# A decoder layer on one Trainium2 core: the order of work at five seams

## The reference

```python
# 1: gated delta rule, 8 heads of 128, two key/value steps for each token
q, k, v = (silu(depthwise_conv4(x @ W.T)) for W in (Wq, Wk, Wv))
state = state * exp(g_t);  v_new = (v_t - k_t @ state) * beta_t
state = state + outer(k_t, v_new);  o_t = q_t @ state
o = rmsnorm(o) * o_norm_w * silu(x @ Wg.T);  x = layernorm(x + o @ Wo.T)
# 2: attention over a 128-row context, 16 heads, rope, a window of 8 keys
# 3: x = layernorm(x + (silu(x @ Wg8.T) * (x @ Wu8.T)) @ Wd8.T), weights dequantized from int32
```

## Time and profile before

| | |
|---|---|
| median of 3 runs | 1237.61 us (1236.98 to 1241.41) |
| profiled execution, its own time | 1236.63 us |
| profiled execution, span of the trace | 1234.6 us, 2.0 us less |
| mean granted TensorE clock | 0.979 |
| PE busy | 1155.6 us, 94% of the span |
| DVE, ACT, POOL busy | 815.0, 716.3, 500.0 us |
| chain that ended last | PE 76%, POOL 6%, DVE 5% |

### The profile page before, as it was taken

How to read it: one execution, slowest core, us unless ns; L and a number is a source line. 1 busy time by engine, 2 the same in 40 slices (tenths; PEclk the granted TensorE clock), 3 DMA queues, 4 the chain that set the end, 5 groups by cost and what they waited for, 6 DMA issues and landing times.

```text
span 1234.6 us, 30002 instructions
## 1 busy us (share of the span) xinstructions
PE 1155.6 (94%) x12192; PEld 794.6 (64%) x12192; DVE 815.0 (66%) x1454; ACT 716.3 (58%) x1212; POOL 500.0 (41%) x709
## 2 busy tenths in 40 slices
PE   6878799999999999999998889859999999999987
PEld 2434455555555555555555556648998988998976
DVE  4878767867768768668675565565666566655552
ACT  4667476767677676676775766533444444444433
POOL 2549575676575674773774811100001100001000
PEclk9899899999999999999998999989999999999999
DMA  3112311412323223243325422161211222111100
GB/s 116 44 38 64 94 49 47 114 55 61 105 57 86 72 60 89 75 130 87 102 60 144 152 61 71 46 232 21 67 44 44 50 51 69 48 44 45 32 17 9
DMA packets 134601, 88.05 MB, mean 71 GB/s; under 512 B 79264, under 2 KB 118048, under 8 KB 133568
## 3 DMA queue, kind: packets, MB, share of 16 engines
q1 hardware_dynamic: 133312, 85.93, 25.7%
q10 hardware_dynamic: 1152, 0.21, 0.1%
HBM read 54.77 MB, written 14.55 MB: 56 GB/s over the span
## 4 chain that ended last, share of the span: by engine, by line
PE 76%; POOL 6%; DVE 5%; SPq 3%; issue 3%; ACT 3%; DMA 3%; ACTq 0%; POOLq 0%; DVEq 0%
PE proj L466 20%; PE out L1484 5%; PE turned_v_chain L1484 4%; PE gram L481 4%; PE proj L1423 4%; PE proj L1542 4%; PE turned_v_chain L1550 4%; PE out L490 2%; PE gram L1458 2%; PE turned_v_chain L595 2%; PE decays L496 2%; DVE conv L986 2%; PE turned_v_chain L628 2%; POOL inverse L1194 2%; PE turned_v_chain L472 2%
## 5 line engine op out<-in xcount | busy, mean ns | idle before, releaser
L986 DVE SCALAR_TENSOR_TENSOR conv<-proj,kq_weights,conv 128x504 f32<-128x504 f32 (+2 forms) x261 | 190.6, 732 | 29.1 <-ACT conv L732 22.3
L466 PE MATMUL proj<-xT,vg_weights 128*128 128x512 f32 x384 | 189.0, 615 | 1.5 <-DMA vg_weights<-in_vg_w 1.4
L1781 POOL TENSOR_TENSOR rope<-rope_part,rope_part 128x512 f32<-128x512 f32 x32 | 40.1, 1272 | 371.0 <-DVE rope_part L1720 371.0
L986 DVE SCALAR_TENSOR_TENSOR conv<-proj,vg_weights,conv 128x504 f32<-128x504 f32 (+2 forms) x192 | 140.9, 734 | 47.7 <-ACT conv L732 42.8
L466 PE MATMUL proj<-xT,kq_weights 128*128 128x512 f32 x348 | 165.4, 601 | 0.4 <-DVE conv L986 0.4
L1194 POOL TENSOR_TENSOR inverse<-inverse,rank_one 128x30 f32<-128x30 f32 (+14 forms) x240 | 126.2, 526 | 18.8
L1191 POOL TENSOR_TENSOR rank_one<-inverse 128x30 f32<-128x30 f32 (+14 forms) x240 | 117.3, 489 | 15.9
L466 PEld LDWEIGHTS proj<-xT,vg_weights 128*128 128x128 f32 x384 | 68.8, 192 | 68.7 <-issue 62.6
L466 PEld LDWEIGHTS proj<-xT,kq_weights 128*128 128x128 f32 x348 | 62.9, 191 | 74.0 <-issue 71.1
L481 PEld LDWEIGHTS gram<-keys_q 128*64 128x64 f32 x896 | 59.1, 141 | 60.3 <-ACT keys_q L743 39.7
L1559 ACT ACTIVATE rstd<-rstd 128x1 f32<-128x1 f32 x48 | 9.7, 202 | 144.2 <-DVE rstd L1667 144.2
(11 more groups left out here) (244 smaller groups left out, 2463.2 us busy)
## 6 DMA issues: line engine op xcount, KB each, us to landing
kq_weights<-in_kq_w SPq DMA_DIRECT2D x32, 390.0 KB, 3.6
vg_weights<-in_vg_w SPq DMA_DIRECT2D x32, 390.0 KB, 4.0
o_scratch<-oT SPq DMA_DIRECT2D x32, 256.0 KB, 2.7
o_in<-o_scratch SPq DMA_DIRECT2D x16, 512.0 KB, 4.1
diagonal<-gram_decayed SPq DMA_DIRECT2D x128, 32.0 KB, 1.9
inverse<-inverse SPq DMA_DIRECT2D x32, 128.0 KB, 2.7
q_first<-rope SPq DMA_DIRECT2D x128, 32.0 KB, 1.9
q_second<-rope SPq DMA_DIRECT2D x128, 32.0 KB, 1.9
```

What stands on the lines that cost most here:

```text
L466: mm = e.matmul(bank(c, u)[:], w[:, (k * 3 + c % 3) * 128:(k * 3 + c % 3 + 1) * 128], xT[g][:, k, :], start=(k == 0), stop=(k == KD - 1))
L986: e.scalar_tensor_tensor(acc(c, u)[:, :, back:], src[:, :, 0:S - back], weights(c, u)[:, j:j + 1], acc(c, u)[:, :, back:], ALU.mult, ALU.a ...
L1781: e.tensor_tensor(turned[half][:].rearrange("p b r q -> p r b q"), parts[2 * half][:], parts[2 * half + 1][:], op).then_inc(s_turned, 1)
```

## The change

Nothing is added or taken away; instructions change places.

1. SP: `load(3)` is issued in slot 41 ahead of the FFN weights, no longer in the loop's first round.
2. Drain, PE: `norm` goes ahead of `chain_y`; in slot 41 `out(2)` goes ahead of `turn_v(0)`.
3. Slot 32, PE: the last `gram(1)` moves from ahead of `output` to behind the projection G.
4. Fill: on PE the projection Q goes ahead of `gram(0)`; on ACT `tap(K1)` goes ahead of the silu of Q, `tap(Q)` ahead of the silu of K1, and `square_q` to the end; on DVE the convolution of Q follows that of K1.
5. Slot 33, DVE: the gate and `oT` go ahead of `solve_norms` and of V0's convolution.

```diff
 SP, slot 41
+                        ahead["load"](3)
                         weights_after_chain()
 PE, slots 1 to 8
+                    e.wait_ge(s_conv[Q], 3 * ua)
+                    project(Q, ua)
                     e.wait_ge(s_silu[Q], ub + 1)
...
                     gram(0, ub)
-                    e.wait_ge(s_conv[Q], 3 * ua)
-                    project(Q, ua)
 PE, drain
+                    if s > U:
+                        norm(ud - 1)
                     if live(uc):
                         chain_y(uc)
-                    if s > U:
-                        norm(ud - 1)
...
+                    if s == last_slot + 1:
+                        ahead["out"](2)
                     if live(ud):
...
                         turn_v(0, ud)
-                    if s == last_slot + 1:
-                        ahead["out"](2)
...
-                    if live(ub):
+                    if live(ua):
                         e.wait_ge(s_gm, 4 * ub + 2)
                         gram(1, ub)
...
                         project(G, uc)
+                        if live(ub) and not live(ua):
+                            e.wait_ge(s_gm, 4 * ub + 2)
+                            gram(1, ub)
 ACT, slots 1 to 8
                         tap(K0, ua)
+                        tap(K1, ua)
                         silu(Q, ub, KQ[ub % 2][:, :, 0:S])
-                    square_q(ub)
-                    tap(K1, ua)
+                    else:
+                        tap(K1, ua)
                     wait(e, s_gram, 2 * (ua - 1))
                     silu(K0, ua, keys(0, ua))
+                    tap(Q, ua)
                     silu(K1, ua, keys(1, ua))
-                    tap(Q, ua)
+                    square_q(ub)
 DVE, fill
                         convolve(K1, ua)
+                        convolve(Q, ua)
...
-                    if s < LAG:
-                        convolve(Q, ua)
-                    elif live(ua):
+                    if s >= LAG and live(ua):
                         convolve(K0, ua)
 DVE, slot 33 (last_batch)
+                    if last_batch:
+                        solve_load(loading, 0)
+                        solve_load(loading, 1)
+                        gate_output()
+                        solve_norms(loading)
+                    if live(uc):
+                        convolve(V0, uc)
 SP, tile loop
-                        if live(u1 + 1):
+                        if live(u1 + 1) and u1 > AHEAD:
                             load(u1 + 1)
```

More of the change, by code:

```diff
@@ L1112, in vector, with gate_output @@
                     last_batch = loading is not None and s > U
-                    if last_batch:
-                        solve_load(loading, 0)
-                        solve_load(loading, 1)
-                        solve_norms(loading)
-                    if live(uc):
-                        convolve(V0, uc)
-                    if loading is not None and not last_batch:
-                        solve_load(loading, 0)
-                    if live(uo):
+                    def gate_output():
                         if s > U:
@@ L1129, in vector @@
                                                ALU.mult).then_inc(s_og, 1)
+                    if last_batch:
[5 more added lines that the diff above has]
+                        convolve(V0, uc)
+                    if loading is not None and not last_batch:
+                        solve_load(loading, 0)
+                    if live(uo) and not last_batch:
+                        gate_output()
                     if live(uc):
```

## The result

| | before | after |
|---|---|---|
| median of the executions timed side by side (4 each) | 1237.62 us (1236.98 to 1241.41) | 1224.14 us (1221.33 to 1228.82) |
| ratio, 95% interval | | 0.9889 (0.9852 to 0.9925) |
| timed a second time (17 and 6 executions), median | 1237.52 us | 1229.45 us, ratio 0.9923 (0.9901 to 0.9946) |
| all executions of this study, mean | 1237.8 us (63) | 1227.2 us (10) |
| profiled execution, span | 1234.6 us | 1219.5 us |

The change makes the kernel faster by about 10.6 us, the difference of the two means (8.6 to 12.6). The first four executions and the first trace of the changed kernel gained more than that; much of the surplus is TensorE's clock, as the experiments show.

The account below looks back on a forecast made before the run. Full slots are PE-bound; only idle PE in fill (12.5 us) and drain (24.0) can be gained. 4.9 + 1.4 + 2.1 + 3.3 = 11.7 us off 1236.6 gives 1225.0; range 1220.5 to 1231.5.

Parts of the forecast that it names:

- the sum with the clock lost everywhere: Whole kernel: with low clock in every term, 4.1 + 1.0 + 2.1 + 2.75 = 10.0 us gained, so 1226.7.
- Fill, 4.9 us: Fill up to the first solve: earlier `decayed(1)`, SP issues and slot 4 weights bring `solve_load` 4.1 to 5.7 us earlier.
- The rival that made the kernel slower: Fill: PE's wait per slot for Q's silu passes 2 us and the clock stays low; 1256.8 us, chance 0.03.
- Behind the first solve, 0: Fill, slots 6 to 8: POOL's elimination sets `steps` for slot 9, so PE waits about 1.3 us; nothing more gained.
- Slot 32, 0: Slot 32: `gram(1)`'s wait goes, but `chain_low` needs DVE behind POOL's elimination and `chain_high` the inverse's DMA; no gain.
- Slots 33 to 36, 1.4: Drain: earlier gate and `oT` remove PE's 1.98 us wait; gain 1.0 to 2.6 us, limited by POOL's last elimination.
- norm over W, 2.1: Slots 37 to 40: `norm` covers three of PE's waits for ACT's copy of W, 0.71 us each.
- All that PE gains in slots 34 to 36 is cut to POOL's 2.6: Slots 34 to 36: POOL's last elimination limits what PE gains there to 2.6 us.
- it probably pays the 1.65 of the low clock once: End of slot 36: PE's wait grows to nearly 3 us, probably costing 1.65 us of low clock once.
- the term for `W_scaled`: Slot 34: `W_scaled` comes 1.4 to 3.4 us earlier, taken as 2.3, from PE's lost wait and G's clock.
- Slot 41, 3.3: Slot 41: `out(2)` fills PE's 3.76 us wait for ACT's ln; gain 2.75 to 3.75 us.
- Tile 3's load, 0: Behind slot 41: `out(3)` waits for DVE's dequantizing, not its load; FFN weights issue about 1.2 us later, no gain.

Follow-up runs that it names:

- Twice Q: Changed kernel with slot 8's Q projection done twice, 1.88 us more PE work: median 1224.64 us, mean 1225.8.
- the move of `steps`: Changed kernel with unit 9's steps behind the first elimination, fill weights issued before the diagonals, and unit 31's `decayed(1)` and `gram(1)` moved: 1221.43 us, ratio 0.9867.
- the diagonals early: Changed kernel with unit 31's `gram(1)` back in its old place and DVE's `decayed(1)` ahead of `solve_turn`: 1221.89 us, ratio 0.9862.
- norm alone: Kernel before with only `norm` ahead of `chain_y` in the drain: 1238.20 us, ratio 0.9999.
- The gate alone: Kernel before with only slot 33's gate and `oT` ahead of `solve_norms`: 1233.82 us, ratio 0.9972.
- the changed kernel again: The changed kernel run once more without an edit, against the kernel before: 1229.45 us, ratio 0.9923.

## Why the prediction came out right, point by point

The mean of the changed kernel's ten executions is 1227.2, 1225.0 was forecast, and 1226.7 stood there as the sum with the clock lost everywhere. Half of the 2.2 us between, 1.2, is the starting point: the forecast took its 11.7 off one execution of 1236.6, and the mean of the kernel before is 1237.8. The fill and slot 41 held; the slots between fell short by 2.6 us. That the first median, 1224.14, lies within 1 us of the forecast is luck: this shortfall was covered by executions that kept more of their clock.

- **Fill, 4.9 us: right.** `solve_load` comes 5.9 us earlier on the mean of six traces against five (73.4, 79.2), the first chain 5.2 (128.9, 134.1). The chain was the one named: DVE's `decayed(1)`, SP's diagonals and constants, the weights. Against an old fill that kept its clock the gain is 4.1, the lower bound that was forecast; against one that lost it, as in the rows of the prediction, 6.9, above the upper bound of 5.7. The 2.8 between them are mostly clock at two places: 1.2 to 1.4 in slot 4, where the forecast had 1.65, and about 1.2 in slot 1, which stood in no term (Q there at 3.4 us, 2.3 in the two others). Two more pieces were too small: Q's tap was there at 43.4 and not 44.9, so SP's chain came 4.2 us earlier, not 3.4, and a regular slot became 0.34 shorter (9.61 us against 9.95), not 0.1 or 0.2. The rival that made the kernel slower did not come: PE's wait for the silu of Q stayed at 1.0 us in these slots.
- **Behind the first solve, 0: right in size, half right in cause.** Twice Q costs nothing, so PE does not bound there. But POOL's elimination is not what the chain waits for at the end, as the move of `steps` shows; `steps` of slot 9, in the middle of it, is. What I left out is the price of the longer wait: at 2.2 us it cost 1.6 or 1.7 us of clock in three of eight traces; the old fill, which hardly waits there, lost none in five.
- **Slot 32, 0:** not tested alone. The moved `gram` let `chain_low` start at 16.26 instead of 17.69 us from the slot's first `chain_y`, and PE then waited for `inverse`, as foretold. What I left out is the move's price on the other side: with `gram(1)` behind G the last diagonals come later, and DVE waits 3.34 us for them ahead of `solve_load` instead of 1.78. With the diagonals early this wait goes.
- **Slots 33 to 36, 1.4, and norm over W, 2.1: this is the step that failed.** "All that PE gains in slots 34 to 36 is cut to POOL's 2.6" fits the first two traces, 2.6 and 2.4 shorter than before (with the diagonals early it is 5.9), and "it probably pays the 1.65 of the low clock once" holds. Together with the W term they were to leave 3.5. Slots 32 to 39 took 133.6 us before and, in the five traces with all drain edits and nothing else in the drain, 134.5, 129.9, 131.9, 133.0 and 134.5, mean 132.8: 0.9 us. Three things failed. First, PE lost its 1.98 us wait for `oT` in slot 33, but waited there for `inverse` (1.0 to 3.0 us in all five) and for V0's convolution (0.8 to 1.6 in four), which now stands behind the gate and the late `solve_load`, and G still ran at 3.2 to 3.8 us in four of the five, where the term for `W_scaled` had it at full clock. Second, where all goes well a covered W wait gives 0.56 and not 0.71 in slots 37 to 39 (51.41 against 52.53, two of them), and V0 at low clock in slot 37, in three of the five, takes 1.8 back. Third, SP's burst in slot 33 is in no term, and neither is the 1.39 us wait of V0 for its weights in slot 35 of the kernel before: it was 3.18 with norm alone, and 1.69 and 2.62 in two of the five, with V0 at the low clock behind it. The gate alone took 132.3 in these slots, so no run shows that `norm` adds anything to it.
- **Slot 41, 3.3: right.** 27.9 to 28.7 us instead of 31.4 to 32.4, 3.6 on the mean; 3.7 by the time of that move alone.
- **Tile 3's load, 0: not tried alone**, but PE's `out(3)` still starts behind DVE's dequantizing, as foretold (at 819.50, where the last dequantizing ends at 819.07). Its 1.6 us in the first trace were not the load's: it takes 6.42 us in the second.

Terms as measured: 5.2 + 0.9 + 3.6 = 9.7, with 0.4 lost in the full slots, against 10.6 by the executions.

## What to carry to other kernels

Where an engine that bounds the kernel waits, price what stands behind the wait as well: here pieces behind 1.3 to 3.8 us of idle PE ran at half clock in part of the executions and at full clock in others. A wait that is covered only helps if the next thing that the engine needs is early too; follow the DMA queue's own order through the stage (a burst of issues is a place in that order) and the slowest chain of the other engines, here the last diagonals. And with a change of under 1%, take ten executions or more and several traces of each: a stage's length in one trace says what it was, not what it is worth. Count every trace with the same order in a stage, also those of kernels that differ elsewhere.

## What the runs showed that I had not expected

- Nearly the same wait at the same place left TensorE's clock at either level. The 63 executions of the kernel before differ by up to 13 us (1231.8 to 1244.9), and time and mean granted clock go together (correlation -0.83 to -0.99 in most kernels; none within the six executions of the changed kernel again, which lie within 3 us).
- One DMA's issue held SP for 4.2 to 6.4 us, behind eleven others, where the like one after it took 0.43. Why this one is not settled.
